# The last two jobs of a two-way row scan: W stationary and the carry moving, and W in plain channel order

## The reference

```python
Wm = W[:, :, (kh - 1) // 2, 0]            # 1024 x 1024, the middle tap
def step(carry, x):
    new = relu(einsum('oc,ncw->now', Wm, carry) + b[None, :, None]) + x
    return (new, new)
xs = moveaxis(fea, 2, 0)                  # rows first
_, ys = lax.scan(step, xs[0], xs[1:])                       # downwards
down = concatenate([xs[:1], ys], axis=0)
_, ys2 = lax.scan(step, down[-1], down[:-1], reverse=True)  # upwards
x = x + moveaxis(concatenate([ys2, down[-1:]], axis=0), 0, 2)
```

## Time and profile before

| | us |
|---|---|
| median of three runs | 1658.34 (1658.21 to 1658.56) |
| span of the profiled execution | 1656.3 |
| TensorE busy in it | 1546.1 (93%) |
| VectorE, ScalarE, GpSimd busy | 1141.4, 1358.5, 960.0 |

### The profile page before, as it was taken

One profiled execution on the slowest core, in us unless ns is written; L12 is line 12 of the kernel. 1 busy time (PEld: TensorE's weight loads), 2 busy tenths in 40 slices (PEclk: granted clock), 3 DMA queues, 4 the chain that ended last, 5 costly groups with the idle time before them and its releaser, 6 DMA issues.

```text
span 1656.3 us, 23710 instructions
## 1 busy us (share of the span) xinstructions
PE 1546.1 (93%) x6812; PEld 1277.0 (77%) x6812; DVE 1141.4 (69%) x3355; ACT 1358.5 (82%) x4265; POOL 960.0 (58%) x1096
## 2 busy tenths in 40 slices
PE   0049999999999999999999999999999999999998
PEld 0037888888888888888888888888888888888886
DVE  5786666766766667666676666766766667666676
ACT  5658888888888888888888888888888888888887
POOL 0066766767667666676675555555555555555554
PEclk9999999999999999999999999999999999999999
DMA  9952323232323232231001444444453535454211
GB/s 406 422 224 77 106 86 115 77 115 77 115 77 115 88 104 96 96 104 50 1 1 54 157 132 155 149 137 152 135 168 119 171 122 166 125 162 135 95 58 58
DMA packets 149555, 207.06 MB, mean 125 GB/s; under 512 B 4016, under 2 KB 135088, under 8 KB 147632
## 3 DMA queue, kind: packets, MB, share of 16 engines
q1 hardware_dynamic: 149280, 205.54, 37.1%
q10 hardware_dynamic: 144, 0.00, 0.0%
HBM read 136.32 MB, written 69.21 MB: 124 GB/s over the span
## 4 chain that ended last, share of the span: by engine, by line
PE 91%; DMA 4%; DVE 3%; ACT 1%; issue 0%; POOL 0%; SPq 0%; ACTq 0%; DVEq 0%
PE bank L640 30%; PE bank L634 30%; PE bank L627 30%; DMA x_ring<-x_groups 4%; DVE turn L476 1%; DVE turn L562 0%; ACT turn L439 0%; DVE d_rows L538 0%; DVE d_rows L535 0%; ACT turn L430 0%; DVE st_lo L542 0%; DVE d_rows L577 0%; DVE moments L501 0%; ACT xn L399 0%; DVE turn L557 0%
## 5 line engine op out<-in xcount | busy, mean ns | idle before, releaser
L627 PE MATMUL bank<-w_hi,st_hi 128*128 128x512 f32 (+1 forms) x2264 | 881.4, 389 | 0.0
L640 PE MATMUL bank<-w_hi,st_lo 128*128 128x512 f32 (+1 forms) x2264 | 880.0, 389 | 0.6 <-DVE st_lo L542 0.3
L634 PE MATMUL bank<-w_lo,st_hi 128*128 128x512 f32 (+1 forms) x2264 | 879.9, 389 | 0.0
L355 POOL TENSOR_TENSOR st_lo<-d_rows,st_hi 128x256 fp32r<-128x256 f32 x650 | 464.0, 738 | 578.0 <-ACT st_hi L448 578.0
L430 ACT ACTIVATE turn<-turn 32x128 f32<-32x128 f32 x2256 | 697.0, 309 | 65.6 <-DVE turn L557 41.6
L562 DVE STREAM_TRANSPOSE turn<-bank 32x128 f32<-32x128 f32 x2256 | 709.6, 315 | 35.5
L640 PEld LDWEIGHTS bank<-w_hi,st_lo 128*128 128x128 f32 (+1 forms) x2264 | 424.2, 187 | 90.8 <-POOL st_lo L355 1.2
L627 PEld LDWEIGHTS bank<-w_hi,st_hi 128*128 128x128 f32 (+1 forms) x2264 | 424.4, 187 | 89.3 <-ACT st_hi L448 0.4
L634 PEld LDWEIGHTS bank<-w_lo,st_hi 128*128 128x128 f32 (+1 forms) x2264 | 424.4, 187 | 89.1 <-issue 0.2
L439 ACT ACTIVATE turn<-turn,bias_sb 128x128 f32<-128x128 f32 (+1 forms) x1132 | 362.4, 391 | 41.8 <-DVE turn L562 3.5
L448 ACT ACTIVATE st_hi<-d_rows 128x256 fp32r<-128x256 f32 x650 | 237.3, 414 | 137.9 <-DVE d_rows L577 137.9
(11 more groups left out here) (45 smaller groups left out, 125.5 us busy)
## 6 DMA issues: line engine op xcount, KB each, us to landing
x_ring<-x_groups SPq DMA_DIRECT2D x82, 768.0 KB, 7.2
out_groups<-x_ring SPq DMA_DIRECT2D x47, 768.0 KB, 5.1
down_rows<-d_rows SPq DMA_DIRECT2D x40, 768.0 KB, 3.8
d_rows<-down_rows SPq DMA_DIRECT2D x40, 768.0 KB, 6.6
x_ring<-x_groups SPq DMA_DIRECT2D x5, 3072.0 KB, 23.6
d_rows<-x_groups SPq DMA_DIRECT2D x4, 3072.0 KB, 23.9
x_ring<-x_groups SPq DMA_DIRECT2D x5, 1536.0 KB, 10.9
d_rows<-w_t SPq DMA_DIRECT2D x16, 256.0 KB, 11.9
```

The source lines that it names most:

```text
L355: final = pool.tensor_tensor(slot(st_lo, at, b * KB, (b + 1) * KB), d_chunk(row_of(i), i % CHUNKS, b * KB, (b + 1) * KB), slot(st_hi, at, ...
L627: return pe.matmul(bank[j % BANKS][0:used(j), :], stationary(st_hi, j, k), w_cols(w_hi, o, k), start=(n == 0), stop=False)
L634: return pe.matmul(bank[j % BANKS][0:used(j), :], stationary(st_hi, j, k), w_cols(w_lo, o, k), start=False, stop=final)
L640: return pe.matmul(bank[j % BANKS][0:used(j), :], stationary(st_lo, j, k), w_cols(w_hi, o, k), start=False, stop=final)
```

## The change

Jobs 281 and 282 (from `TURNED` on) are done the other way round. The stationary operand is a block of 128 x 128 of W, and the carry moves. Hi and lo of the carry now lie in one tile, so that one matmul takes w_hi with both (256 columns in job 281, 128 in job 282) and a second takes w_lo with hi (128 and 64). Each of a job's four blocks of 128 output channels has a PSUM bank of its own, with channels on the partitions, so nothing is turned. A finished block is worked on by itself: ScalarE reads the half with lo and adds the bias, VectorE adds the other half, takes the maximum with 0 and adds the row, and adds that to x in the ring. After each two blocks SP stores a piece, four pieces in all. GpSimd's last addition is the lower half of step 280. W is in plain channel order, so `turn_blocks` and `move_blocks` of the other 281 jobs read their blocks in four runs.

```diff
-LAST_PIECES = ((0, 2), (2, 4))
+LAST_PIECES = ((4, 6), (6, 8), (0, 2), (2, 4))
+TURNED = JOBS - 2
-        st_hi = sb("st_hi", [P, K, (SLOTS + 1) * Q], F32R)
-        st_lo = sb("st_lo", [P, K, (SLOTS + 1) * Q], F32R)
+        st = sb("st", [P, K, 2, (SLOTS + 1) * Q], F32R)
+        st_hi, st_lo = st[:, :, 0, :], st[:, :, 1, :]
         def source(t, q, u):
-            return t[q * B32:(q + 1) * B32, u * P:(u + 1) * P].rearrange("p (k a) -> p k a", k=KB)
+            return t[q * B32:(q + 1) * B32, :].rearrange("p (k e) -> p k e", k=KB)[:, :, u * B32:(u + 1) * B32]
...
+            def end_products(j, kk):
+                o = j % 2
+                acc = end_bank(j, kk)
+                pe.wait_ge(direct_done, TURNED + KB * (j - TURNED) + kk - BANKS + 1)
+                for n in range(K):
+                    k = KB * blocks_of(j)[n // KB] + n % KB
+                    if kk == 0:
+                        wait_split(hi_ready, first_hi, j, n)
+                        wait_split(lo_ready, first_lo, j, n)
+                    pe.matmul(acc[:, 0:2 * used(j)], w_block(w_hi, o, k, kk), carried(j, k), start=(n == 0), stop=False)
+                    done = pe.matmul(acc[:, 0:used(j)], w_block(w_lo, o, k, kk), carried(j, k)[:, 0, :],
+                                     start=False, stop=(n == K - 1))
+                done.then_inc(block_ready, 1)
...
+            for j in range(TURNED, JOBS):           # ScalarE
+                for kk in range(KB):
+                    k = (j % 2) * KB + kk
+                    act.wait_ge(block_ready, KB * (j - TURNED) + kk + 1)
+                    act.activation(end_made(j, kk), end_bank(j, kk)[:, used(j):2 * used(j)], ACT.Identity,
+                                   bias=bias_sb[:, k:k + 1]).then_inc(low_biased, 1)
...
-                dve.transpose(blocks[0:used(j), :], bank[j % BANKS][0:used(j), 0:ACT_QUADS * P]).then_inc(blocks_ready, 1)
+                whole = bank[j % BANKS][0:used(j), :].rearrange("p (k e) -> p k e", k=KB)[:, :, 0:ACT_QUADS * B32]
+                dve.transpose(blocks[0:used(j), :].rearrange("p (k e) -> p k e", k=KB), whole).then_inc(blocks_ready, 1)
...
+            def end_block(j, kk):
+                b = j % 2
+                n = used(j)
+                product, made = end_bank(j, kk), end_made(j, kk)
+                carry, there = end_row(j, b * KB + kk)
+                done = KB * (j - TURNED) + kk + 1
+                dve.wait_ge(low_biased, done)
+                dve.tensor_tensor(made, product[:, 0:n], made, ALU.add).then_inc(last_made, 1)
+                dve.wait_ge(last_made, 2 * done - 1)
+                dve.scalar_tensor_tensor(out=made, in0=made, scalar=0.0, in1=carry, op0=ALU.max, op1=ALU.add
+                                         ).then_inc(last_made, 1)
+                dve.wait_ge(last_made, 2 * done)
+                dve.tensor_tensor(there, there, made.rearrange("p (c n w) -> p c n w", n=NI, w=W16), ALU.add
+                                  ).then_inc(last_out, 1)
...
-            sp.wait_ge(out_ready, CHUNKS * H)
-            sp.dma_start(row_in(out_groups, 0, KB, K), ring_row(0, KB, K)).then_inc(out_stored[0], 16)
+            sp.wait_ge(out_ready, CHUNKS * H - 1)
             for n, (k0, k1) in enumerate(LAST_PIECES):
-                sp.wait_ge(last_out, n + 1)
+                sp.wait_ge(last_out, 2 * (n + 1))
                 sp.dma_start(row_in(out_groups, 0, k0, k1), ring_row(0, k0, k1)).then_inc(out_stored[0], 16)
...
-    w_t = by_quadrant(w[:, :, tap, 0].T).reshape(K, P, C_)
+    w_t = np.ascontiguousarray(w[:, :, tap, 0].T).reshape(K, P, C_)
```

More of the change, by code:

```diff
@@ L198, in stationary, with w_block, carried, end_bank @@
             return st[:, k, at * Q:at * Q + used(j)]
+        def w_block(w, o, k, kk):
+            return w_cols(w, o, k)[:, kk * P:(kk + 1) * P]
+        def carried(j, k):
+            at = places(members(j)[0])[-1]
+            return st[:, k, :, at * Q:at * Q + used(j)]
+        def end_bank(j, kk):
+            return bank[(TURNED + KB * (j - TURNED) + kk) % BANKS]
+        def end_made(j, kk):
+            return xn[:, j - TURNED, kk * P:kk * P + used(j)]
+        def end_row(j, k):
+            c = members(j)[0] % CHUNKS
+            return (d_ring[:, 0, :].rearrange("p (k e) -> p k e", k=K)[:, k, c * Q:c * Q + used(j)],
+                    x_ring[:, k, 0, :].rearrange("p (n c w) -> p c n w", n=NI, c=CHUNKS)[:, c:c + len(members(j))])
         def source(t, q, u):
-            return t[q * B32:(q + 1) * B32, u * P:(u + 1) * P].rearrange("p (k a) -> p k a", k=KB)
+            return t[q * B32:(q + 1) * B32, :].rearrange("p (k e) -> p k e", k=KB)[:, :, u * B32:(u + 1) * B32]
         def target(j, q, u):
@@ L253, in build @@
         last_out = sem("last_out")
+        block_ready = sem("block_ready")
+        low_biased = sem("low_biased")
         block = ctx.enter_context(nc.Block())
@@ L303, in _ @@
                                  ).then_inc(x_loaded[above % RING], 16)
-            sp.wait_ge(out_ready, CHUNKS * H)
-            sp.dma_start(row_in(out_groups, 0, KB, K), ring_row(0, KB, K)).then_inc(out_stored[0], 16)
+            sp.wait_ge(out_ready, CHUNKS * H - 1)
             for n, (k0, k1) in enumerate(LAST_PIECES):
-                sp.wait_ge(last_out, n + 1)
+                sp.wait_ge(last_out, 2 * (n + 1))
                 sp.dma_start(row_in(out_groups, 0, k0, k1), ring_row(0, k0, k1)).then_inc(out_stored[0], 16)
             for r in range(RING):
-                sp.wait_ge(out_stored[r], 16 * (GROUPS if r else GROUPS + len(LAST_PIECES)))
+                sp.wait_ge(out_stored[r], 16 * (GROUPS if r else LAST + len(LAST_PIECES)))
         @block.gpsimd
@@ L341, in output @@
                     pool.wait_ge(x_loaded[h % RING], 16 * (LAST + (H - 1 - h) // RING))
-                if i == STEPS - 1:
+                if i == TURNED - 1:
                     pool.wait_ge(y_ready, first_done(i))
-                    pool.tensor_tensor(x_chunk(h, c, KB, K), x_chunk(h, c, KB, K), by_image(d_chunk(h, c, KB, K)),
+                    pool.tensor_tensor(x_chunk(h, c, 0, KB), x_chunk(h, c, 0, KB), by_image(d_chunk(h, c, 0, KB)),
                                        ALU.add).then_inc(out_ready, 1)
@@ L361, in _ @@
                 normalise(i)
-            for j in range(JOBS):
+            for j in range(TURNED):
                 for i in members(j):
@@ L367, in _ @@
                     normalise(j + XN_AHEAD)
-                if DOWN - CHUNKS <= j - 1 < STEPS - 1:
+                if DOWN - CHUNKS <= j - 1:
                     output(j - 1)
-            output(STEPS - 1)
+            output(TURNED - 1)
         @block.scalar
@@ L439, in rectify @@
                     final = act.activation(cols, cols, ACT.Relu, bias=bias_sb[:, k:k + 1])
-                    if j == JOBS - 1 and kk + 1 == LAST_PIECES[0][1]:
-                        final.then_inc(rectified, 1)
                 final.then_inc(rectified, 1)
@@ L577, in make_half @@
                 dve.tensor_tensor(here, product_of(j, i), addend, ALU.add).then_inc(y_ready, 1)
-            for j in range(JOBS - 1):
+            for j in range(TURNED):
                 turn_blocks(j)
@@ L583, in _ @@
                     make_half(j, i)
-            turn_blocks(JOBS - 1)
-            c = CHUNKS - 1
+            def end_block(j, kk):
[12 more added lines that the diff above has]
+                                  ).then_inc(last_out, 1)
             dve.wait_ge(d_loaded[0], 16 * LAST)
             dve.wait_ge(x_loaded[0], 16 * 2 * LAST)
[L589 to L595, removed]
+            for j in range(TURNED, JOBS):
+                for kk in range(KB):
+                    end_block(j, kk)
         @block.tensor
@@ L654, in _ @@
             done.then_inc(acc_ready, 1)
-            for j in range(2, JOBS):
+            for j in range(2, TURNED):
                 if j >= BANKS:
@@ L663, in _ @@
                 done.then_inc(acc_ready, 1)
+            def end_products(j, kk):
[11 more added lines that the diff above has]
+                done.then_inc(block_ready, 1)
+            for j in range(TURNED, JOBS):
+                for kk in range(KB):
+                    end_products(j, kk)
 def kernel(x, L0_conv_W, L0_conv_b):
@@ L672 @@
     tap = (w.shape[2] - 1) // 2
-    def by_quadrant(a):
-        lead = a.shape[:-1]
-        split = a.reshape(lead + (2, KB, QUADS, B32))
-        return np.ascontiguousarray(np.swapaxes(split, -3, -2)).reshape(lead + (C_,))
     x_groups = np.ascontiguousarray(x.reshape(N, K, P, GROUPS, RING, W).transpose(3, 2, 1, 4, 0, 5)
                                     ).reshape(GROUPS, P, K * RING * N * W)
-    w_t = by_quadrant(w[:, :, tap, 0].T).reshape(K, P, C_)
+    w_t = np.ascontiguousarray(w[:, :, tap, 0].T).reshape(K, P, C_)
     bias = np.ascontiguousarray(b.reshape(K, P).T)
```

## The result

The changed kernel takes 1661.58 us (median of 13 runs, 1660.03 to 1662.53), the kernel before, measured beside it, 1658.29 us (13 runs, 1658.20 to 1658.56). The ratio is 1.0018, with a 95% interval of 1.0011 to 1.0025: 3.3 us slower. That is at the edge of what the prediction held to be told from no change, but no run of one kernel lies among those of the other. The likeliest time of the prediction was 1659.0, its range 1655.9 to 1666.0. What was not there before is the scatter: 2.5 us between executions, against 0.4 us.

The account below looks back on a forecast made before the run. TensorE was taken to bound the kernel, busy 93% of the span. TensorE's +3.21 us less 2.52 us of tail gave +0.69 us on the median 1658.34: 1659.0, own range 1658.6 to 1660.6, range with rivals 1655.9 to 1666.0.

Parts of the forecast that it names:

- Loads set the pace: TensorE, jobs 281 and 282: a load-bound matmul costs 0.107 us, other end 0.120; 14.11 us for both jobs before the stall.
- The fast-loads rival: Jobs 281 and 282: streams set the pace and VectorE becomes the bound, 1655.9 us; at the skill's 81 ns, 1656.5; chance 0.12.
- dear short streams: Rival, jobs 281 and 282: short streams of this number format cost more, 20.9 us for both, 1665.8 us; chance 0.13.
- loads in the open: Rival, jobs 281 and 282: each load runs before its stream, unhidden, 21.9 us, 1666.8 us, or 1669; chance 0.07.
- The stall for the carry's second half: TensorE in job 281, after 8 short matmuls: waits for GpSimd's split of the carry, 0.06 us with the semaphore.
- The tail: From the last matmul to the last addition: 1.22 us in place of 3.74, shrinking by 2.52 us.
- VectorE waits for TensorE at the end: Last two jobs: VectorE keeps up, job 282's blocks coming every 1.71 us and needing 0.75 us of VectorE.
- The reshaped reads cost nothing: Earlier 281 jobs: reading four runs costs at most 0.04 us a job, under the 0.18 us of slack.
- The clock falls: Rival, job 282: clock drops to 1.2 GHz half way through, 3.4 us more, 1662.4 us; chance 0.07.

Follow-up runs that it names:

- the second experiment: The kernel before with W in plain order, reads in four runs and the merged carry tile, jobs 281 and 282 as before: 1658.33 us.
- the first experiment: The changed kernel with job 282 streaming 256 and 128 columns, the added columns' products read by nobody: 1659.61 us.
- the seventh experiment: The changed kernel with only the hi part moved under w_hi in job 282, so both matmuls of a pair stream 64 columns: 1663.26 us.
- the same experiment: The kernel before with only job 282 turned round, its streams widened to 256 and 128 columns: 1658.15 us.

## Why the prediction was right and where it was not

The measured 1661.58 us lies in the range, but that is owed to the rivals that the range took in: the forecast's own range ended at 1660.6.

*Loads set the pace: right.* 0.107 us were forecast, with 0.120 as the other end; 0.112 was measured, with 128 and 64 columns and with 64 and 64 alike, and 0.115 on average with 256 and 128. The fast-loads rival falls with it: the Trainium skill's 81 ns (TensorE: Matmul & The Clock Gate, Back-to-back issue gap) was not reached, and the measurement decides. So do the rivals of dear short streams and of loads in the open.

*The stall for the carry's second half:* 0.06 us forecast, 0.22 measured. GpSimd was done at 1640.17, so 0.14 us passed between its end and the matmul. Small, but four times the forecast.

*The tail: right.* 1.22 us forecast, 1.12 measured.

*VectorE waits for TensorE at the end: right* for the changed kernel (1.79 us before its last block). I had not seen that GpSimd's additions would hold VectorE up in the middle: job 281's four blocks were forecast to end at 1648.35 and ended at 1649.27, of which 0.28 us is the later start. In the changed kernel that is hidden, and with job 281 as before it is not.

*The reshaped reads cost nothing: right*, by the second experiment.

*The clock: wrong, and this is 2.2 of the 2.6 us between 1659.0 and 1661.58.* The forecast priced every load at the full clock, and the prediction gave "The clock falls" 0.07, on the ground "that TensorE issues without a pause". It fell without a pause, in the profiles of all three kernels whose job 282 streams no more than 128 columns at a time, and not in those of the kernels that stream 256 and 128. The mean granted clock of every run agrees: 0.996 to 0.998 and once 0.999 in the first three, 0.999 or 1.000 in the others. With the clock held, the first experiment gives 1659.61, of which by my estimate 0.2 us is its wider streams (32 x (0.230 - 0.223)): 1659.4 for the change as it was forecast, against 1659.0, the rest being 0.005 us on most of the loads and the longer stall. By this estimate the fall costs the median execution 2.2 us, where the rival had 3.4 us for a fall half way through. The rival had foreseen the fall, and its chance was too low: no row showed that a TensorE busy with loads keeps its clock.

What decides when the clock falls in an execution stays open; the profiles show 6 us, 5 us and 3 us after job 282's start, one execution each. Which property of the thin streams brings it down is not shown either: the first and the seventh experiment changed their width and nothing else.

## What to carry to other kernels

When the small operand moves and the large one is loaded, count loads: with 128 columns loaded for each matmul, in this number format, the pace was 0.112 us whether 64 or 128 columns moved and 0.115 us with 128 and 256 by turns, while the clock may be lost. If the streams are thin, widening them with columns that nobody reads can be cheaper than leaving them thin (1659.6 against 1661.6 us). And when a tail is rebuilt, look at each bound that stands behind the first: here TensorE, then VectorE beside GpSimd, then the stores, within 1 us of each other; only the last job done the new way, with the additions taken out of its path, made a gain of 0.9 us, with an interval that still takes in none.

## What was not expected of the hardware

TensorE's clock fell from 2.4 to 1.2 GHz with weight loads back to back, a load every 0.112 us and a matmul behind each. Moving 64 or 128 columns it fell, in the profiled executions of three kernels; moving 256 and 128 columns by turns, at nearly the same pace of loads (0.115 us), it stayed at 1.00 to the last matmul. And a VectorE step of 0.23 us took 0.93 us beside a GpSimd addition of 1.32 us, where the one with an input in PSUM, 1650.05 to 1650.27 in the same experiment, did not stretch.
